# A recommender's first layer: a quarter of the embedding features looked up by matmuls with rows of ones and zeros

## What is computed

```python
F, V, D, B = 32, 1000, 64, 1024
H1, H2, OUT = (1024, 512, 1000)
e = emb_tables[jnp.arange(F)[None, :], x]
gram = jnp.einsum('bid,bjd->bij', e, e)
iu, ju = jnp.triu_indices(F, k=1)
cross = gram[:, iu, ju]
h = jnp.concatenate([e.reshape(B, F * D), cross], axis=1)
h = jax.nn.relu(h @ W1 + b1)
h = jax.nn.relu(h @ W2 + b2)
logits = h @ W3 + b3
return jax.nn.sigmoid(logits)
```

## Time and profile before

| | |
|---|---|
| median of 3 runs | 668.47 us (664.09 to 670.59) |
| profiled execution, first to last instruction | 660.4 us |
| a run shown, less that span | 3.7 to 10.2 us, 8.1 for the median |
| mean granted clock of TensorE | 0.852 |

### The profile page before, as it was taken

One profiled execution on the slowest core, in us unless ns is written; L12 is line 12 of the kernel. 1 busy time (PEld: TensorE's weight loads), 2 busy tenths in 40 slices (PEclk: granted clock), 3 DMA queues, 4 the chain that ended last, 5 costly groups with the idle time before them and its releaser, 6 DMA issues.

```text
span 660.4 us, 8819 instructions
## 1 busy us (share of the span) xinstructions
PE 456.6 (69%) x3344; PEld 434.9 (66%) x3344; DVE 291.9 (44%) x461; ACT 246.6 (37%) x449; POOL 269.1 (41%) x265
## 2 busy tenths in 40 slices
PE   0222137572759876676799899811799999999786
PEld 0012127471749876576699889811799899999786
DVE  6210024150324553253546658610546688846641
ACT  3110023130334342152534666500434776834532
POOL 6777717577540377767100378777000000000000
PEclk9997558585769888768699999955799999999989
DMA  6611101131316211332086424411175305186522
GB/s 195 217 51 26 26 6 23 21 95 52 99 33 251 75 25 22 88 102 71 15 288 187 126 58 116 120 26 26 76 262 177 104 23 164 66 279 188 161 90 63
DMA packets 29145, 67.60 MB, mean 102 GB/s; under 512 B 6418, under 2 KB 12722, under 8 KB 28594
## 3 DMA queue, kind: packets, MB, share of 16 engines
q1 hardware_dynamic: 16834, 54.54, 25.7%
q0 software_dynamic: 8192, 8.40, 6.2%
q10 hardware_dynamic: 4080, 4.10, 2.1%
HBM read 56.63 MB, written 10.39 MB: 101 GB/s over the span
## 4 chain that ended last, share of the span: by engine, by line
PE 51%; another core or an unknown queue 17%; issue 11%; DVE 6%; POOL 5%; ACT 5%; DMA 4%; SPq 0%; ACTq 0%
PE h1p L491 11%; PE h1p L493 10%; PE h1p L492 10%; PE misc L524 8%; POOL emb L255 5%; PE misc L491 3%; PE misc L492 3%; PE misc L493 3%; DVE dg L418 2%; PE misc L513 2%; DVE h1p L435 2%; DMA out_dram<-res 2%; ACT whi L299 1%; ACT z L304 1%
## 5 line engine op out<-in xcount | busy, mean ns | idle before, releaser
L255 POOL DMA_INDIRECT emb<-tables_dram,idx x256 | 267.4, 1045 | 184.9 <-PE misc L513 101.7
L491 PE MATMUL h1p<-xhi,whi 128*128 128x256 f32 x512 | 156.4, 306 | 16.8 <-issue 12.7
L493 PE MATMUL h1p<-xhi,wlo 128*128 128x256 f32 x512 | 151.2, 295 | 12.5 <-issue 12.2
L492 PE MATMUL h1p<-xlo,whi 128*128 128x256 f32 x512 | 151.2, 295 | 8.7 <-issue 8.6
L524 PE MATMUL misc<-z 128*128 128x128 f32 x512 | 78.8, 322 | 89.5 <-ACT dg L315 50.3
L524 PEld LDWEIGHTS misc<-z 128*128 128x128 f32 x512 | 74.2, 233 | 93.7 <-ACT dg L315 51.6
L400 DVE TENSOR_TENSOR wlo<-wraw,whi 128x1024 fp32r<-128x1024 f32 (+1 forms) x80 | 97.2, 1215 | 60.7 <-ACT whi L299 60.2
L491 PEld LDWEIGHTS h1p<-xhi,whi 128*128 128x128 f32 x512 | 104.3, 204 | 18.2 <-issue 13.8
L492 PEld LDWEIGHTS h1p<-xlo,whi 128*128 128x128 f32 x512 | 104.1, 203 | 13.9 <-issue 13.6
L493 PEld LDWEIGHTS h1p<-xhi,wlo 128*128 128x128 f32 x512 | 103.8, 203 | 12.6 <-issue 12.2
L299 ACT CAST whi<-wraw 128x1024 fp32r<-128x1024 f32 (+1 forms) x80 | 84.1, 1052 | 57.6 <-PE h1p L493 34.4
(11 more groups left out here) (39 smaller groups left out, 589.1 us busy)
## 6 DMA issues: line engine op xcount, KB each, us to landing
wraw<-w_dram SPq DMA_DIRECT2D x64, 512.0 KB
wraw<-w_dram SPq DMA_DIRECT2D x16, 500.0 KB
wres<-w_dram SPq DMA_DIRECT2D x8, 512.0 KB, 3.6
emb<-tables_dram,idx POOLq DMA_INDIRECT x256
gram_scratch<-dg SPq DMA_DIRECT2D x4, 1024.0 KB, 3.9
out_dram<-res ACTq DMA_DIRECT2D x16, 250.0 KB
gram_scratch<-dg SPq DMA_DIRECT2D x4, 512.0 KB, 4.8
gc<-gram_scratch SPq DMA_DIRECT2D x16, 128.0 KB, 2.8
```

Of the source, the lines that this page charges most:

```text
L255: nc.gpsimd.indirect_dma_start(emb[:, k, t, f * D:(f + 1) * D], None, tables, bass.IndirectOffsetOnAxis(ap=idx[:, t, 2 * k + f:2 * k + f + ...
L491: nc.tensor.matmul(dst, whi[:, slot, cols], hi, start=start, stop=False, skip_group_check=True)
L492: nc.tensor.matmul(dst, whi[:, slot, cols], lo, start=False, stop=False, skip_group_check=True)
L493: return nc.tensor.matmul(dst, wlo[:, slot, cols], hi, start=False, stop=stop, skip_group_check=True)
```

## The change

32 features become 24 gathered and 8 looked up. The features are renumbered in pairs by tile, tiles 12 to 15 are looked up.

- **Looking up.** The 1000 rows of a table are laid as 125 partitions x 8. POOL compares a broadcast row of indices with the row numbers: 8 operations for one feature and block ("a half"), each 125x256, into hot (three copies). The table chunk takes the place of a weight chunk in the ring, its high and low parts side by side, and 8 matmuls per feature (125 rows, 128 columns, 256 moving) leave high and low part of the embedding in PSUM. ACT and DVE copy and add them.
- **Order.** `schedule()` writes all four blocks out; a tile is transposed two at a time, and layer 1 follows each pair of tiles at once. emb has two copies of 12 tiles. POOL mixes the halves among the gathers by `gathers_before`.
- **Weights.** All W1 chunks are streamed in each block (no wres); 32 steps a block instead of 28. DVE subtracts in four pieces of 256 columns.
- **Inner products.** z uses all 128 partitions (128 samples' tile t in each half of them). A product is 64x64 (two samples) on 64 rows, 128 products a block instead of 64; copies take 512 numbers per partition instead of 128.
- **Scratch.** The second write goes; the four reads have 31 rows each, and the last row of gc stays at one, which carries the bias b1 as a weight row.
- **Outputs.** SP issues them instead of ACT. Relu of h1 is ACT's, the low part a single DVE operation from PSUM.

The core of the diff:

```diff
-RESIDENT = 8
-XRING = 8
+GP = 6
+GT = 2 * GP
+LOOKS = KT - GT
+VP, VC = 125, 8
+HOTS = 3
+LEAD = 24
+XRING = 16
+AHEAD = 3
+LOADS_AHEAD = 6
+def schedule():
...
+    yield ("look", 0, 12)
+    for n in range(BLOCKS):
+        yield ("tr", n, 0)
+        yield from emb(n, 12, 0)
+        yield ("look", n, 13)
+        yield from emb(n, 1)
+        yield from l2(n - 1, 0)
+        yield ("tr", n, 1)
...
+        yield ("tr", n, 4)
+        yield from emb(n, 5)
+        yield from l3(n - 1, 2)
+        yield ("tr", n, 5)
+        yield from emb(n, 15, 6)
+        yield ("gram", n)
+        yield from emb(n, 7, 8)
+        yield ("move", n)
+        yield from emb(n, 9)
+        yield from l3(n - 1, 3)
+        yield from emb(n, 10)
+        yield ("pairs", n)
+        yield from emb(n, 11)
+        for k in range(CROSS):
+            yield ("pair", n, k)
+        yield ("h1", n)
+        if n + 1 < BLOCKS:
+            yield ("look", n + 1, 12)
...
+def gathers_before(h):
+
+    n, at = divmod(h, 2 * LOOKS)
+    if n == 0:
+        return (0, 0, 4, 8, 18, 24, 28, 32)[at]
+    return min(BLOCKS * 4 * GT, 4 * GT * n + LEAD - 10 + 6 * at)
...
-                sp.dma_start(gd[:, 0:F, :], dg[:]).then_inc(s_gdw, 16)
-                sp.dma_start(gd[:, F:GROW, :], dg[:, 0:F // 2, :]).then_inc(s_gdw, 16)
...
-                                  ap=[[(GROW + 1) * QB, F], [F * GROW * QB, 4], [1, CROSS * QB]])
-                    sp.dma_start(gc[F * kk:F * (kk + 1), :, :, :].rearrange("i c t q -> i c (t q)"),
+                if kind == "gram":
+                    if n > 0:
+                        sp.wait_ge(s_gc, 64 * n)
+                    sp.wait_ge(s_dga, GROUPS * (n + 1))
+                    sp.wait_ge(s_dgv, GROUPS * (n + 1))
+                    sp.dma_start(gd, dg[:]).then_inc(s_gdw, 16)
+                if kind == "move":
+                    sp.wait_ge(s_gdw, 16 * (n + 1))
...
+                    for kk in range(4):
+                        src = bass.AP(tensor=gd.tensor, offset=(CROSS * kk + 1) * QB,
+                                      ap=[[(F + 1) * QB, F - 1], [F * F * QB, 4], [1, CROSS * QB]])
+                        sp.dma_start(gc[F * kk:F * (kk + 1) - 1, :, :, :].rearrange("i c s q -> i c (s q)"),
+                                     src).then_inc(s_gc, 16)
...
+                src = bass.AP(tensor=xt.tensor, offset=2 * k * B + n * NB, ap=[[0, VP], [B, 2], [1, NB]])
+                sp.dma_start(xb[0:VP, i % 2, :, :], src).then_inc(s_xb[i % 2], 16)
...
+            def ones(h):
+
+                i, f = divmod(h, 2)
+                pool.wait_ge(s_xb[i % 2], 16 * (i // 2 + 1))
+                if h >= HOTS:
+                    pool.wait_ge(s_used, used_after(*LOOKED[(h - HOTS) // 2]))
+                for c in range(VC):
+                    last = nc.gpsimd.tensor_scalar(hot[0:VP, h % HOTS, c, :], xb[0:VP, i % 2, f, :],
+                                                   vals[0:VP, c:c + 1], None, ALU.is_equal)
+                last.then_inc(s_hot, 1)
...
+                if n >= 2 and (k % 2, t, f) == (0, 0, 0):
+                    pool.wait_ge(s_t, GP * (n - 2) + m + 1)
...
+                for i in range(4):
+                    part = slice(w // 4 * i, w // 4 * (i + 1))
...
+                        last = nc.vector.tensor_tensor(wlo(u % RING)[:, part], wraw[:, u % RAWS, part],
+                                                       whi(u % RING)[:, part].bitcast(fp32), ALU.subtract)
...
+            def look_up(n, k, slot):
+                i, a = SLOT["look", n, k], LOOK["look", n, k]
+                slot_free(i, n)
+                for f in range(2):
+                    pe.wait_ge(s_hot, 2 * a + f + 1)
+                    for c in range(VC):
+                        last = nc.tensor.matmul(misc[:, i % 2, NB * f:NB * (f + 1)],
+                                                wsplit[0:VP, slot, P * (VC * f + c):P * (VC * f + c + 1)],
+                                                hot[0:VP, (2 * a + f) % HOTS, c, :], start=(f, c) == (0, 0),
+                                                stop=c == VC - 1, skip_group_check=True)
+                return last
...
+                    for q in range(8):
+                        for h in range(2):
+                            for t in range(BT):
+                                zq = z[D * t:D * (t + 1), 8 * g + q, 2 * h:2 * h + 2, :].rearrange("d c f -> d (c f)")
+                                last = nc.tensor.matmul(misc[D * h:D * (h + 1), 2 * (g % 2) + t, D * q:D * (q + 1)],
+                                                        zq, zq, start=True, stop=True)
+                    last.then_inc(s_gram, 1)
```

More of the change, by code:

```diff
@@ L32, in recsys_kernel, with used_after, grams_before, outs_before @@
     ACT = mybir.ActivationFunctionType
[L36 to L75, removed]
+    ITEMS = list(schedule())
+    STEPS = [item for item in ITEMS if item[0] in ("emb", "pair", "l2", "l3", "look")]
+    STEP = {item: u for u, item in enumerate(STEPS)}
+    SLOT = {item: i for i, item in enumerate(item for item in ITEMS if item[0] in ("tr", "look"))}
+    LOOK = {item: i for i, item in enumerate(item for item in ITEMS if item[0] == "look")}
+    LOOKED = list(LOOK)
+    OUTS = [item for item in ITEMS if item[0] == "out"]
+    def used_after(*item):
+        return STEP[item] + 1
+    def grams_before(*item):
+        return sum(o[0] == "gram" for o in ITEMS[:ITEMS.index(item)])
+    def outs_before(item):
+        return sum(ITEMS.index(o) < ITEMS.index(item) for o in OUTS)
+    gd = nc.dram_tensor("gram_scratch", [4 * F, F, QB], fp32, kind="Internal").ap()
     ctx = ExitStack()
@@ L149, in recsys_kernel, with width, whi, wlo @@
         s_sig = sem("s_sig")
-        s_out = [sem(f"s_out{k}") for k in range(2)]
+        s_out = [sem(f"s_out{j}") for j in range(2)]
         block = ctx.enter_context(nc.Block())
[L156 to L177, removed]
+        def width(kind):
+            return OUT if kind == "l3" else H1
+        def whi(slot, w=H1):
+            return wsplit[:, slot, 0:w]
+        def wlo(slot, w=H1):
+            return wsplit[:, slot, H1:H1 + w]
+        def table_part(slot, half):
+            return wsplit[0:VP, slot, :].rearrange("p (g h d) -> p g h d", h=2, d=D)[:, :, half, :]
+        def table_raw(u):
+            return wraw[0:VP, u % RAWS, :].rearrange("p (g d) -> p g d", d=D)
+        def chunk_in_dram(kind, n, k):
             if kind == "emb":
@@ new lines, in _ @@
+            made = 0
+            gathers = [(n, k, t, f) for n in range(BLOCKS) for k in range(GT) for t in range(BT) for f in range(2)]
+            for g, (n, k, t, f) in enumerate(gathers):
+                while made < 2 * len(LOOKED) and gathers_before(made) <= g:
+                    ones(made)
+                    made += 1
+                m = k // 2
+                if g == 0:
+                    pool.wait_ge(s_idx, 1)
+                if (n, k, t, f) == (1, 0, 0, 0):
+                    pool.wait_ge(s_idx, 2)
+                if n >= 2 and (k % 2, t, f) == (0, 0, 0):
+                    pool.wait_ge(s_t, GP * (n - 2) + m + 1)
+                nc.gpsimd.indirect_dma_start(
+                    emb[:, n % 2, k, t, f * D:(f + 1) * D], None, tables,
+                    bass.IndirectOffsetOnAxis(ap=idx[:, BT * n + t, 2 * k + f:2 * k + f + 1], axis=0),
+                ).then_inc(s_emb[n % 2][m], 16)
@@ L301, in even_to_z @@
[L301 to L318 removed]
+            act.wait_ge(s_const, 48)
@@ L599, in layer3 @@
                 return last
-            run(FIRST, BODY, 0, None, 0)
-            with pe.Fori(1, BLOCKS - 1) as n:
-                run(BODY, BODY, n, n - 1, first_seq(n))
-            n = BLOCKS - 1
-            run(BODY, LAST, n, n - 1, first_seq(n))
-            run(LAST, [], None, n, first_seq(BLOCKS))
+            for kind, n, *k in ITEMS:
+                if kind == "tr":
+                    transposes(n, k[0])
+                if kind == "gram":
+                    gram(n)
+                if (kind, n, *k) in STEP:
+                    u = STEP[kind, n, k[0]]
+                    pe.wait_ge(s_wlo, u + 1)
+                    if kind in ("emb", "pair"):
+                        last = layer1(kind, n, k[0], u % RING)
+                    elif kind == "look":
+                        last = look_up(n, k[0], u % RING)
+                    elif kind == "l2":
+                        last = layer2(n, k[0], u % RING)
+                    else:
+                        last = layer3(n, k[0], u % RING)
+                    last.then_inc(s_used, 1)
 def pair_rows():
```

649 lines of the change are left out of this document (328 added, 321 removed).

## The result

The changed kernel takes 698.37 us (median of 4 runs, 698.07 to 699.11), the kernel before beside it 669.53 (4 runs, 664.09 to 670.74): a ratio of 1.046, interval 1.040 to 1.052. It is slower, and 64 us over the forecast, outside its range of 530 to 690. The profiled execution has a span of 696.5 us.

A forecast was written before the change was run, and what follows sets the result against it. The prediction took the kernel as bound by a chain through the gathers for its first 460 us, then by TensorE. Block 0 186, blocks 1 to 3 402, tail 38 make 626, and 8: 634 us, range 530 to 690.

The forecast's parts named there:

- Rows of ones and zeros: POOL's 256 comparisons for the lookup: 0.6 us each, 4.8 us a half, 38 us a block.
- rival 2: The ones are slow and POOL is the bound: 1.25 us per comparison, wait included, 736 us in all; chance 0.14.
- POOL's 110 lies beside: In blocks 1 to 3, POOL's gathers and comparisons, 110 us a block, run beside the block's 134 us.
- POOL's ones: Comparisons held up, through s_used, behind the gc wait, pair steps and next block's lookup; no size given.
- the tail: The end of the run: 38 us after the blocks in the prediction's sum; the ledger's 53 starts at block 3's gc.
- the 8 between span and run: Added to the sum of 626 us because the earlier span was 660.4 us against a median of 668.5.
- unbroken gathers 32 to 61: In block 0 these gathers come without a break and hold TensorE up: 6 us added.
- the gram: Inner products on TensorE, 256 instructions of 64 columns a block: 14 us, between 7 and 28.
- TensorE's 104 us a block: Lookup 7.6, transposes 2.6, steps of layers 1 to 3 79.5 and gram 14 us, summed per block.
- The four gc loads: Scratch reads of 31 rows each, all on one DMA engine: 31 us to land, between 9 and 40.
- Rival 1: The gc load is fast, spread or on separate engines: 532 us in all; chance 0.22.
- Rival 3: Gathers go on holding TensorE up, 0.48 us per gather, 69 us for 144: 669 us, no change; chance 0.06.

The follow-up runs named there:

- e9: The changed kernel with only four of each eight comparisons (128 instead of 256 on GpSimd): 586.9 us beside a before of 497.7, ratio 1.178.
- e17: The changed kernel, unchanged, where the kernel before takes 498.0 us: 669.4 us, ratio 1.343.
- e1: The changed kernel with each gc load of 31 rows issued as 16 and 15 rows: 614.5 us beside a before of 663.2, ratio 0.927.
- e4: The kernel before with each 32-row gc load issued as 31 rows and one row: 746.0 us beside a before of 663.2.
- e16: The kernel of e11 run again, where the kernel before takes 659.1 us: 512.4 us, ratio 0.782.
- e11: e8 with block 0's comparisons all on DVE and one 1000-column fill after every fourth gather there: 508.2 us beside a before of 497.7, ratio 1.020.
- e13: The changed kernel, unchanged, where the kernel before takes 660.2 us: 700.7 us, ratio 1.059.
- e6: The changed kernel with gc loads as 16 and 15 rows, comparisons on DVE, a one-column fill after every fourth gather: 635.9 us beside a before of 666.3.
- e5: The changed kernel with gc loads as 16 and 15 rows, comparisons on DVE, two 1000-column fills after every fourth gather: 537.1 us beside a before of 666.3.
- e8: e1 with even features' comparisons singly between gathers on GpSimd, odd features' on DVE: 538.5 us beside a before of 666.3, ratio 0.813.

## Why the prediction was wrong

**The size of one term, and where it stood.** "Rows of ones and zeros" took 0.6 us for a comparison, between 0.377 and 0.961 by the iota and the add; it measured 0.998 in the mean, above my upper bound and at rival 2's turning point of 0.98. Where DVE subtracts no weights it is 0.906, inside my bounds. So of the 0.4 us missing from my 0.6, 0.3 is this base price, and 0.1 in the mean is what comes on top beside DVE's subtractions. I had scaled it from rows of 64 columns of other operations, one of them without input. "POOL's 110 lies beside" then failed: its work is 125 us, and it is not free to run beside TensorE, since its ones wait for a copy of hot that the lookup after the pair steps frees. I had written that very wait down ("POOL's ones", behind the waiting instructions) and not added it to POOL's sum: 125 and 28 are the 153 measured for a block, where I had 134. e9 shows that the size is what failed: there the ones cost POOL 33 us a block (I had forecast 38, the change has 63), and the period is 133.

**The ledger**, by the times at which gc has landed and ACT starts on it (forecast from the prediction's sum, less the 2.3 us of ACT and DVE: 171, 305, 439, 573; measured 202.8, 356.6, 509.9, 649.6; the tail 53 and 46.9). Block 0: 32 late. Blocks 1 and 2: 20 and 19 (153.8 and 153.3 for 134). Block 3: 6. Tail: 6 early. 32 + 20 + 19 + 6 - 6 = 71, 696.5 less 626; the 8 between span and run that I added were 2. (My 8 compared the span of one execution with the median of others; in every run on record time and span differ by some 1.8 us.)

**Block 0.** Gather 47 ends at 128.5 us, forecast 104: its eight halves of ones take 60.5 us (7.6 each) instead of 38.4, 22 of the 24.5 by which it is late. I added 6 for unbroken gathers 32 to 61; they cost 23.5 (gc ready at 202.8 here, at 179.3 in e17 without the hold-up). Against it, the gram took 6.3 us a block (1024 instructions, 25.3 us), below the 7 I gave as its lower bound and far below 14. TensorE's 104 us a block is met all the same (104.7 and 106.3 busy between POOL's rows), which is luck: the 8 us of the gram are made up for by steps that run partly at the lower clock (0.83 and 0.82 granted in the mean).

**What was right.** The four gc loads: TensorE was forecast to stand still 26, 23, 23 and 23 us; it waited 80.5 us in all, ACT 24.5, 21.1, 20.9 and 19.9; e1 and e4 move the time by 84 and 83 us by this alone. The Trainium skill's rule ("DMA: Bandwidth & Descriptors", "Why a DMA increments its semaphore by 16 and not by 1") makes the number of engines the largest divisor up to 16 of the rows, 1 for 31 and 16 and 15 for e1's parts. By it e1's loads had to be fast, and its waits for gc (4.4 us at most) agree. DVE's four pieces overlap more than I took (0.36 us apart, 1.43 a weight for 1.65), at no effect.

**The rivals.** Rival 1 did not come. Rival 2 is what happened by its sign; its formula at 1.0 us gives 6 + 288 + 256 + 114 + 8 = 672, for 698 measured (669 without the hold-up). That it comes near is luck: gathers at 1.27 with issue instead of 1.5 are 44 us less, POOL's waits of 85 us, which it left out, are more, and tail and launch were 13 less. Rival 3 came in block 0 (23.5 of the 27.5 us by which gc's last load is later than in e17); its price per gather does not hold: the same kernel with a broken stream takes 512.4 us with the hold-up (e16) and 508.2 without (e11).

**The gain that was expected.** It was there and was given back. Without the hold-up before is 498 and after 669: the change costs 171 us by itself. The hold-up costs before 162 us (660 less 498) and after 31 (700.7 less 669.4). On chips with it, 171 lost less 131 saved shows as 40, as in e13. My sum started from a before of 668 without asking whether 160 of it were one phenomenon with its own conditions.

## What to carry to other kernels

Count the rows of each transfer: 31 rows cost 20 us more than 16 + 15, and whatever shares the ring pays too. An engine whose buffers are freed by another's late step is in series with it: write its period as work plus wait before calling it hidden. Where gathers run in an unbroken stream, look at TensorE's instructions beside them; if they come 1.4 us apart, break the stream after every fourth by about 1 us of other work or by waiting, and measure on more than one chip before believing a gain.

## What the runs showed of the hardware that I had not expected

- The same program takes 659 to 670 us on some chips and 498 on others (medians), with the same gathers in 40:60 (17, 15.1 us). On the former, an unbroken stream of indirect gathers slows TensorE to one instruction in 1.4 us or more; it ends when the stream is broken by a fill of 0.95 us in four gathers (e16), not by one of 0.12 that leaves the gathers 1.25 us apart (e6). Whether it comes from the chip, its state or the tracing is open: all runs here were traced.
- A comparison of 125x256 int32 with a column of scalars takes 0.998 us on GpSimd in the mean (0.906 where VectorE subtracts no weights, up to 1.08 where it does) and 0.37 on VectorE (0.43 to 0.45 with more beside it in e5 and e8).
- An instruction of an fp32 product of 64x64 (two make one product) takes 25 ns on TensorE in the mean of the changed kernel, and 18 ns at a granted clock of 1.00 (128 in 2.31 us in e17), where one of 128x128 takes 110 ns in the earlier trace rows at the same clock.
